# A graph network block: the adjacency's scatter as a straight list, and the folded linear product ahead of the masked attention's loop

## The reference

```python
xn = _layernorm(x)
q, k, v = xn @ Wq + bq, xn @ Wk + bk, xn @ Wv + bv
adj = zeros((N, N)).at[src, dst].set(1.0)        # 33792 edges
a = q @ k.T / sqrt(512)
a = a * adj + (1.0 - adj) * -1e6
x = x + softmax(a) @ v                            # masked attention
# a linear "attention" without softmax, heads of 64:
x = x + (einsum(q2, k2) * SCALE / n, v2) @ w_out + b_out
...
x = x + switch_ffn(_layernorm(x))                 # 16 experts
x = x + gnn(...) + splat_attention(_layernorm(x)) # layer 1
x = x + moe(_layernorm(x))
```

## Time and profile before

| | |
|---|---|
| median of 3 runs | 1317.12 us (1316.8 to 1320.16) |
| profiled execution | 1318.35 us |
| its span, first to last instruction | 1316.5 us |
| busy: TensorE, VectorE, ScalarE, GpSimd | 882.7, 531.5, 342.9, 421.3 us |
| mean granted TensorE clock | 0.829 of full speed |

### The profile page before, as it was taken

One profiled execution on the slowest core, in us unless ns is written; L12 is line 12 of the kernel. 1 busy time (PEld: TensorE's weight loads), 2 busy tenths in 40 slices (PEclk: granted clock), 3 DMA queues, 4 the chain that ended last, 5 costly groups with the idle time before them and its releaser, 6 DMA issues.

```text
span 1316.5 us, 11299 instructions
## 1 busy us (share of the span) xinstructions
PE 882.7 (67%) x3882; PEld 602.4 (46%) x3882; DVE 531.5 (40%) x855; ACT 342.9 (26%) x514; POOL 421.3 (32%) x407
## 2 busy tenths in 40 slices
PE   4902000131019899999991993899998678898978
PEld 2502000120017688887870432677765434444565
DVE  5400000110012367406654118632245678764377
ACT  1200000100000244223220112121332057788521
POOL 5777777776630000000003105400000035456401
PEclk9955555565557899999996995999999879998999
DMA  9501000310000000300123974010100000000001
GB/s 342 201 0 32 0 0 0 120 41 0 0 0 0 1 0 0 128 0 33 61 100 105 309 272 128 27 64 0 64 0 1 33 1 0 2 2 1 1 5 64
DMA packets 45599, 70.51 MB, mean 54 GB/s; under 512 B 12577, under 2 KB 13729, under 8 KB 45554
## 3 DMA queue, kind: packets, MB, share of 16 engines
q1 hardware_dynamic: 33266, 60.39, 13.8%
q0 software_dynamic: 10752, 6.90, 2.0%
q10 hardware_dynamic: 1536, 2.62, 0.6%
HBM read 58.22 MB, written 11.67 MB: 53 GB/s over the span
## 4 chain that ended last, share of the span: by engine, by line
PE 55%; another core or an unknown queue 24%; DVE 12%; ACT 3%; issue 3%; DMA 2%; POOL 1%; SPq 0%; ACTq 0%; DVEq 0%; PEldq 0%; POOLq 0%
PE bank L782 11%; PE bank L784 10%; PE bank L783 10%; PE bank L930 6%; PE bank L998 4%; PE bank L838 2%; DVE key L1848 2%; PE bank L1081 1%; PE bank L1112 1%; PE bank L886 1%; ACT slot L1192 1%; DVE cols L1451 1%; DVE xT L1445 1%; PE bank L1053 1%
## 5 line engine op out<-in xcount | busy, mean ns | idle before, releaser
L720 POOL DMA_INDIRECT not_adjacent<-zero,keyring x264 | 263.8, 999 | 99.5 <-issue 85.6
L782 PE MATMUL bank<-slot 128*128 128x512 f32 (+1 forms) x212 | 88.1, 415 | 187.4 <-issue 156.6
L762 POOL TENSOR_TENSOR slot<-arena,slot 128x512 fp32r<-128x512 f32 x43 | 66.6, 1549 | 274.3 <-ACT slot L1366 274.0
L782 PEld LDWEIGHTS bank<-slot 128*128 128x128 f32 x212 | 43.5, 205 | 198.4 <-issue 166.3
L1445 DVE TENSOR_TENSOR slot<-bank,slot 128x512 fp32r<-128x512 f32 x44 | 29.2, 687 | 249.4 <-issue 151.9
L1198 ACT ACTIVATE slot<-bank 128x512 fp32r<-128x512 f32 x60 | 35.0, 597 | 363.4 <-remote 184.0
L735 POOL DMA_INDIRECT expert_rows<-xn,idx x8 | 8.3, 1037 | 329.2 <-DVE idx L1712 327.1
L782 PE MATMUL bank<-xT,slot 128*128 128x512 f32 (+1 forms) x248 | 105.0, 423 | 7.7 <-DVE xT L1445 5.8
L783 PE MATMUL bank<-slot 128*128 128x512 f32 (+1 forms) x212 | 85.5, 403 | 21.7 <-issue 21.7
L784 PE MATMUL bank<-slot 128*128 128x512 f32 (+1 forms) x212 | 85.3, 402 | 20.2 <-issue 20.2
L783 PE MATMUL bank<-xT,slot 128*128 128x512 f32 (+1 forms) x248 | 97.7, 394 | 0.0
(11 more groups left out here) (276 smaller groups left out, 1651.4 us busy)
## 6 DMA issues: line engine op xcount, KB each, us to landing
arena<-in_ewT SPq DMA_DIRECT2D x16, 1024.0 KB, 8.8
arena<-in_edge_attr SPq DMA_DIRECT2D x3, 2816.0 KB, 24.1
not_adjacent<-zero,keyring POOLq DMA_INDIRECT x264
wraw<-in_qkvT SPq DMA_DIRECT2D x3, 1024.0 KB
expert_rows<-rowb SPq DMA_DIRECT2D x1, 2560.0 KB
wraw<-in_L_ffn_expert_b POOLq DMA_DIRECT2D x16, 160.0 KB, 5.8
expert_results<-wraw ACTq DMA_DIRECT2D x16, 160.0 KB, 5.8
not_adjacent<-agg SPq DMA_DIRECT2D x1, 2048.0 KB, 8.4
```

Source lines behind the costliest of these rows:

```text
L720: pool.indirect_dma_start(adjd, bass.IndirectOffsetOnAxis(ap=keyring[:, h, b:b + 1], axis=0), zero16[:, :], None).then_inc(scattered[h], 16)
L762: pool.tensor_tensor(psplit(n % 3, 1, 1), pexp[:, n % 3, 1, :], f32(psplit(n % 3, 0, 1)), ALU.subtract).then_inc(p_lo[1], 1)
L782: pe.matmul(out, L[1], R[0], start=start, stop=False, **kw)
```

## The change

The loop over batches, the copies to `keyring` and the two counts that go with them are gone; all 264 indirect DMAs are written out, take their keys from `key` itself, and the wait for batch q - 2 is on a constant. The linear branch gets products of its own, `XB`, 8 of 12 matmuls, behind the 8 `V` products and ahead of the loop; VectorE adds them to `xres`. `AV` then holds the probabilities' part alone. mask(0), mask(1), scale(0) and exponential 0 stand behind all of `V`, on VectorE behind all additions of `XB` as well.

```diff
@@ -125,6 +125,8 @@
             add("S", it, jh)
     for t in range(T):
         add("V", t)
+    for t in range(T):
+        add("XB", t)
     for t in range(T):
         add("PT", t, 0, bank=2 * (t % 2))
         add("PT", t, 1, bank=2 * (t % 2) + 1)
@@ -296,7 +298,6 @@
         rowb = sb("rowb", [P, D])
         agg = sb("agg", [P, T, EA])
         cols = sb("cols", [P, 176])
-        keyring = sb("keyring", [P, 2, BATCH], U32)
         zero16 = sb("zero16", [P, 1], U16)
         spans = sb("spans", [P, 2, NCH])
         plan = sb("plan", [1, 2, T], I32)
@@ -412,8 +413,6 @@
         buf_cleared = sem("buf_cleared")
         keys_ready = sem("keys_ready")
         dst_ready = sem("dst_ready")
-        key_copied = sem("key_copied")
-        batch_ready = sem("batch_ready")
         scattered = [sem(f"scattered{i}") for i in range(2)]
         adj_in = [sem(f"adj_in{t}") for t in range(T)]
         xres_in = sem("xres_in")
@@ -711,22 +710,12 @@
             pool.wait_ge(adj_cleared, 16)
             pool.wait_ge(keys_ready, 1)
 
-            def scatter_half(i, h):
-
-                pool.tensor_copy(keyring[:, h, :], key[:, bass.ds(i * (2 * BATCH) + h * BATCH, BATCH)]).then_inc(key_copied, 1)
-                pool.wait_ge(key_copied, i * 2 + (h + 1))
-                pool.sem_inc(batch_ready, 1)
-                for b in range(BATCH):
-                    pool.indirect_dma_start(adjd, bass.IndirectOffsetOnAxis(ap=keyring[:, h, b:b + 1], axis=0),
-                                            zero16[:, :], None).then_inc(scattered[h], 16)
-
-            for h in range(2):
-                scatter_half(0, h)
-            with pool.Fori(1, SCATTERS // (2 * BATCH)) as i:
-                for h in range(2):
-
-                    pool.wait_ge(scattered[h], i * (16 * BATCH))
-                    scatter_half(i, h)
+            for q in range(SCATTERS // BATCH):
+                if q >= 2:
+                    pool.wait_ge(scattered[q % 2], q // 2 * (16 * BATCH))
+                for j in range(q * BATCH, (q + 1) * BATCH):
+                    pool.indirect_dma_start(adjd, bass.IndirectOffsetOnAxis(ap=key[:, j:j + 1], axis=0),
+                                            zero16[:, :], None).then_inc(scattered[q % 2], 16)
 
             pool.wait_ge(buf_cleared, 16)
             pool.wait_ge(route_ready, 1)
@@ -947,10 +936,14 @@
             pe.wait_ge(w_split, windex["Wv"] + 1)
             for t in range(T):
                 product(("V", t), lambda k: xt(t, k), lambda k: sl(3, k))
-            for t in range(T):
-                emptied(pe, "V", t)
             for m in range(C):
                 emptied(pe, "B", m)
+            for t in range(T):
+                product(("XB", t), lambda k: xt(t, k), lambda k: sl(1, k))
+            for t in range(T):
+                emptied(pe, "V", t)
+            for t in range(T - 4, T):
+                emptied(pe, "XB", t)
 
             for t in range(T):
                 pe.wait_ge(p_ready, t + 1)
@@ -961,14 +954,12 @@
                         ins = pe.transpose(o[:, chunk(j)], scores[:, t, jt * P:(jt + 1) * P], ident)
                     close(ins)
                 o = open_bank("AV", t)
-                for k in range(C):
-                    mm3(o, xt(t, k), sl(1, k), k == 0, False)
                 for g in range(2):
                     emptied(pe, "PT", t, g)
                     for j in range(4):
                         jt = 4 * g + j
                         ins = mm3(o, hl(slot[3], 2 * (t % 2) + g, chunk(j)), sl(2 * (jt // TH), jt % TH),
-                                  False, jt == T - 1)
+                                  jt == 0, jt == T - 1)
                 close(ins)
 
 
@@ -1268,8 +1259,7 @@
 
             for t in range(T):
                 hi(("V", t))
-                if t == 5:
-                    exponentials(0)
+            exponentials(0)
             for t in range(T):
                 for g in range(2):
                     if t >= 2:
@@ -1625,13 +1615,15 @@
 
             for t in range(T):
                 lo(("V", t))
-                if t == 4:
-                    mask(0)
-                if t == 5:
-                    mask(1)
-                if t == 6:
-                    scale(0)
             dve.wait_ge(bias_added, 1)
+            for t in range(T):
+                finished(dve, "XB", t)
+                dve.tensor_tensor(xres[:, t, :], at("XB", t), xres[:, t, :], ALU.add).then_inc(evicted[bank_of[("XB", t)]], 1)
+            mask(0)
+            mask(1)
+            scale(0)
+            for t in range(T - 4, T):
+                emptied(dve, "XB", t)
             for t in range(T + 1):
                 if t < T:
                     for g in range(2):
```

More of the change, by code:

```diff
@@ L949, in _ @@
                 product(("V", t), lambda k: xt(t, k), lambda k: sl(3, k))
+            for m in range(C):
+                emptied(pe, "B", m)
+            for t in range(T):
+                product(("XB", t), lambda k: xt(t, k), lambda k: sl(1, k))
             for t in range(T):
                 emptied(pe, "V", t)
-            for m in range(C):
-                emptied(pe, "B", m)
+            for t in range(T - 4, T):
+                emptied(pe, "XB", t)
             for t in range(T):
```

## The result

| | before | after |
|---|---|---|
| median of 4 runs | 1316.96 us | 1336.96 us (1332.98 to 1337.2) |
| span of the profiled execution | 1316.5 us | 1335.0 us |

The ratio is 1.0138 (95%: 1.012 to 1.0156): 20 us slower, where I forecast no change. The time is inside the range; the sign is the one I gave 0.34.

The account below looks back on a forecast made before the run. The prediction took slow TensorE completions during the scatter to bound the first 384 us, and masked attention the second stretch. The shorter scatter's -15 and the moved product's +15 summed to 0: 1317 us, range 1275 to 1345.

Parts of the forecast that it names:

- the sign is the one I gave 0.34: Whole kernel: chance 0.34 of slower, against 0.41 for faster and 0.25 for the same.
- The crawl: TensorE's completions come through slowly during the scatter, 1.4 to 2.9 us per matmul; said to bound the first 384 us.
- The scatter ends at 358.3: GpSimd's indirect DMAs: without batch boundaries the last one ends 20.6 us earlier, at 358.3 in place of 378.9.
- I take 15: TensorE's gain from the shorter scatter, B 3 known earlier: 15 us, with ends 0 and 20.6.
- The product in front, 26.85 later: Ahead of the attention loop: with XB behind V, tile 0's transposes start near 634.6 in place of 607.75.
- The loop 60.4 us: Masked-attention loop: five passes of 7.7 us, VectorE setting the period, and three of 7.3, against 72.8 before; 12.4 back.
- my end of +18: Upper end for moving XB in front of the loop: forecast +15 us, ends +12 and +18.
- Rival 1: Scatter stretch: the crawl stays and ends with the scatter; 1317 us, from 1309 to 1335; chance 0.62.
- part 1: The scatter's part of the change: last DMA 20.6 us earlier, gain taken as 15 us; nothing if the crawl isn't tied to it.
- Rival 2: Scatter stretch: the crawl goes because the scatter loop caused it, and the scatter becomes the bound; 1072 us; chance 0.16.
- Rival 3: Scatter stretch: the crawl stays but its pace rises, from fewer counts and no copies; 1230 to 1300 us; chance 0.10.
- Rival 4: Scatter stretch: the crawl's pace falls, as the gapless scatter has 5% more DMAs per us; 1337 us; chance 0.12.

Follow-up runs that it names:

- list_only: Kernel before with only the scatter loop replaced by the straight list of indirect DMAs: 1319.0 us, ratio 1.0013 to the kernel before.
- masks_under_b: Changed kernel with mask(0), mask(1) and scale(0) put behind VectorE's additions of XB 3, 4 and 5: 1331.1 us, ratio 1.0247 to the kernel before.
- product_only: Changed kernel with the old scatter loop, key copies and key ring put back: 1334.4 us, ratio 1.010 to the kernel before.
- sets B and E: Two groups of follow-up runs, each on one chip with the kernel before beside it; there that kernel took 1106.5 and 1106.4 us.
- after_b: Changed kernel, unchanged, run again in a set without the crawl: 1076.9 us, ratio 0.9734 to the kernel before.
- pause_double: Kernel before with the straight scatter list and two fills and waits ahead of every indirect DMA: 1163.9 us, one run, against 1303.6.
- after_double_b: Changed kernel with two fills and waits ahead of every indirect DMA, in a set with the crawl: 1146.6 us, ratio 0.869 to the kernel before.

## Why the prediction was wrong, step by step

- **The crawl is the bound of the first 384 us**: right, and the largest thing in this kernel. Whole sets without it are 212 us shorter, 1106 against 1318 for the kernel before.
- **The scatter ends at 358.3**: right, 355.7. The sum had two dear batch boundaries in the trace before; there are three, and the third, 3.05 us ahead of the DMA at 310.87, makes up most of the 2.6 us.
- **"I take 15" for what this brings TensorE**: this is the step that failed. It rested on the crawl's lasting as long as the scatter; the profile before showed the two ends 5 us apart, and I called that the strongest thing seen. The runs showed a backlog in its place: it is done 1.40 us per DMA after the first, at 383, whether the last DMA is issued at 356 or 378. The lower bound that I had kept, 0, was the value (`U` starts 0.03 us earlier, and `list_only` has nothing measurable). The number was to be had from the trace before: 264 DMAs in 366 us are 1.39 us each, but 1.27 within a batch. The two coincide because the kernel before issued, with its boundaries, at almost the rate of the service. A shorter scatter made the backlog larger, not its end earlier.
- **The product in front, 26.85 later**: right, 26.8.
- **The loop 60.4 us**: off by 4.7. The first pass took 9.85 us in place of 7.3, with the clock at the lower level in its first part (0.50 of full speed from 633.4 to 639.2); the next five 7.8 to 8.0 in place of 7.7, the last two 7.8 and 7.9 in place of 7.3. And "VectorE now sets the period" was wrong: the rows of TensorE show no wait ahead of the second and all later transposes, so the period is TensorE's own. Its pieces are 2.1 to 2.2 us in place of 1.8 from the transposes to the first `AV` matmul, and 5.7 to 5.8 in place of 5.45 for the 24 matmuls. Masks under `XB` (`masks_under_b`) removed the idle stretch and left the loop at 64.6. The sum of this part is +19.1, above my end of +18; `product_only` measured +16.
- **Together**: -1 + 19 = +18, where I had -15 + 15; the -1 is the 1.1 us in front of the move, which aren't the scatter's. The median moved by 20.
- **Rival 1** held in kind (the crawl stays), with its price from the end "nothing" of part 1: 1317 + 18 = 1335. I gave that corner too little, since 15 of 20.6 seemed likeliest. **Rival 2's** time, 1072, is near what the changed kernel takes where the crawl is absent (1076.9), but the loop didn't cause the crawl: `list_only` has it in full, and the kernel before lacks it in sets B and E. **Rival 3**: the pace stayed. **Rival 4** gave 1337 by a slower pace; the pace stayed at 2.8 us, so the agreement of the number is chance.

The prediction named a section of the Trainium skill, "NOTIFIC — the notification-queue block", "7.1 Overflow: three behaviours, one of which stalls the engine": the block that writes event records holds its producers back rather than lose a record inside itself. By it the scatter's completions would cause the crawl, and the crawl would stay. It did stay, and even steps fit a slow service: from 104.67 to 372.07 us the starts of ScalarE's high parts in the changed kernel are whole multiples of 0.70 us apart (33.60, 8.40, 7.00 and others). But records were also lost, not only held back. The trace of the changed kernel holds 4738 records of semaphore updates with the crawl, and 8702 in `after_b` without it. Nearly all that are missing are landings of DMAs, 2541 against 6436. In `pause_double` and `after_double_b` there are 5788 and 5412, so some are missing at 1.61 us as well. The crawl and the loss of records go together; that one causes the other, and what the block has to do with it, no run here shows.

Open: what switches the crawl on for all runs of a set and off for the next on the same chip. Every time here comes from an execution that the profiler recorded, so whether a kernel that nobody records crawls at all wasn't tried. Open too is whether it is a DMA's counts or something else of it that needs the 1.40 us.

## What to carry to other kernels

When an engine waits for nothing but another's completions, and these come in even steps, compute a rate: what else produces completions at that time, how many, and how far apart. Two ends that coincide are no proof that one causes the other; ask what a third quantity, number times service time, gives. And it may pay to slow down a source that nobody waits for: 1.61 us between background DMAs, in place of 1.39 on average, went with a kernel 11 to 13% faster where the backlog stood, in recorded executions.

Moving a product out of a loop is worth what the wait is that it lands in: behind the crawl it cost 16 to 19 us, in a wait for the scatter it was free.

## What the runs showed of the hardware

- In the sets with the crawl, beside 264 indirect DMAs of 128 keys 1.27 us apart, TensorE's completions came one in 2.8 us until 1.40 us per DMA had passed (383 us; 198 us with 132 DMAs). 1.43 us apart they did so in stretches. 1.61 us apart that pace was gone, with 29 us of delay left in the edge loop. In the sets without the crawl the same list, most of its DMAs 1.27 us apart, held nothing up.
- The same kernel on the same chip took 1105.6 to 1108.6 us in the seven runs of one set and 1316.0 to 1320.5 in the seven of another. A comparison holds only within a set: the change is 1.4% slower in one kind and 2.7% faster in the other.
- TensorE's granted clock was at the lower level (0.50) for 2.8 us after two waits of 1.09 and 1.17 us close together in `masks_under_b`; a single wait of 1.07 us in the next pass left it at 1.00.
